# A two-layer graph kernel on one core: 32768 for the dynamic transfers' scratch, f32 one-hots, no room of its own for xin

## What is computed

```python
# layer 0: Z is x (12500, 256), U (4, 256, 16), Dmat (256, 256)
ZU = jnp.einsum('nd,kdr->knr', Z, U)
zs = ZU[:, src, :]
zd = ZU[:, dst, :]
logits = (zs * zd).sum(-1) / 4
seg_max = segment_max(logits, dst)              # per head
exp_l = jnp.exp(logits - seg_max[:, dst])
alpha = exp_l / (segment_sum(exp_l, dst)[:, dst] + 1e-16)
agg = segment_sum(alpha[..., None] * zs, dst)
w = jax.nn.softmax(head_w)
ssa = jnp.einsum('k,knr,kdr->nd', w, agg, U)
Z_half = 0.5 * Z + 0.5 * ssa
residual = Z_half - (Z_half @ Dmat.T) @ Dmat
x = layernorm(x + relu(Z_half + 0.5 * (residual @ Dmat) - 0.05))
# layer 1: xt = (x @ weight).reshape(-1, 4, 64); alpha from xt[row] and xt[col]
tmp = jnp.einsum('nh,nhd->nd', alpha[:n], xt[col[:n]])   # broadcast over the 4 heads
x = layernorm(x + broadcast(tmp))
```

## Time and profile before

| | |
|---|---|
| median of 3 runs | 3771.14 us (3765.44 to 3793.86) |
| the profiled execution | 3755.32 us, span 3753.5 us, mean granted clock 0.572 |
| PE busy | 1961.4 us (52%), 15249 products |
| PE's weight loads | 1492.6 us (40%) |
| DVE busy | 1919.1 us (51%) |
| ACT busy | 1169.7 us (31%) |
| POOL busy | 1721.7 us (46%) |
| prologue, edge loop | 0 to 178 us, 178 to 3301 us |
| dense stage, layer 1 | 3301 to 3412 us, 3412 to 3753 us |

### The profile page before, as it was taken

How to read it: one execution, slowest core, us unless ns; L and a number is a source line. 1 busy time by engine, 2 the same in 40 slices (tenths; PEclk the granted TensorE clock), 3 DMA queues, 4 the chain that set the end, 5 groups by cost and what they waited for, 6 DMA issues and landing times. The chain is left out here.

```text
span 3753.5 us, 61674 instructions
## 1 busy us (share of the span) xinstructions
PE 1961.4 (52%) x15249; PEld 1492.6 (40%) x15250; DVE 1919.1 (51%) x5861; ACT 1169.7 (31%) x3041; POOL 1721.7 (46%) x1833
## 2 busy tenths in 40 slices
PE   7344545454555445445445455354444554594776
PEld 7233434333343333333334334243333333453665
DVE  6344545445555445545455455455445544682566
ACT  2012222323323232323223232223232323353557
POOL 3544454444444444444444444544544444224662
PEclk8555555555555555555555555555555555597877
DMA  6211211121221212211112112121211121293343
GB/s 208 52 37 38 48 42 43 39 46 41 48 47 43 44 40 45 47 40 44 42 38 46 42 41 47 41 48 41 47 38 44 40 47 38 65 314 115 120 139 98
DMA packets 406592, 232.96 MB, mean 62 GB/s; under 512 B 284096, under 2 KB 371434, under 8 KB 406506
## 3 DMA queue, kind: packets, MB, share of 16 engines
q1 hardware_dynamic: 346666, 154.11, 15.0%
q0 software_dynamic: 59840, 77.87, 9.7%
HBM read 134.80 MB, written 42.55 MB: 47 GB/s over the span
## 5 line engine op out<-in xcount | busy, mean ns | idle before, releaser
L549 POOL DMA_INDIRECT arena<-z_table,sslot x1563 | 1487.8, 952 | 1702.9 <-SPq L400 1191.5
L1303 PE MATMUL bank<-arena 128*128 x4992 | 609.5, 228 | 564.2 <-issue 474.7
L1538 ACT ACTIVATE arena<-bank 128x272 f32<-128x272 f32 x416 | 268.4, 662 | 1614.6 <-remote 983.0
L1303 PEld LDWEIGHTS bank<-arena 128*128 128x128 bf16 x4992 | 469.3, 107 | 708.9 <-issue 616.4
L850 DVE TENSOR_TENSOR xin<-arena,bank 128x512 f32<-128x512 f32 x208 | 142.9, 687 | 1034.3 <-remote 697.3
L1515 ACT ACTIVATE acc<-xTb 128x68 f32 x1600 | 386.6, 312 | 350.1 <-issue 339.6
L1320 PE MATMUL bank<-xto,arena 128*128 128x68 bf16 x3328 | 330.7, 246 | 218.9 <-issue 218.8
L1320 PE MATMUL bank<-arena 128*128 128x68 bf16 x1664 | 300.3, 244 | 211.1 <-issue 135.0
L1320 PEld LDWEIGHTS bank<-xto,arena 128*128 128x128 bf16 x3328 | 284.7, 132 | 242.1 <-issue 241.7
L1291 PE MATMUL bank<-ident_b,arena 128*128 128x128 bf16 x1664 | 211.0, 306 | 317.9 <-remote 132.1
L841 DVE TENSOR_SCALAR arena<-iota_b,didx 128x128 bf16<-128x128 bf16 x1664 | 302.0, 264 | 40.8 <-issue 34.2
(11 more groups left out here) (250 smaller groups left out, 2493.2 us busy)
## 6 DMA issues: line engine op xcount, KB each, us to landing
arena<-arena SPq DMA_DIRECT2D x1660, 32.0 KB
arena<-z_table,sslot POOLq DMA_INDIRECT x1563
dspace<-in_xT SPq DMA_DIRECT2D x49, 256.0 KB
xmz_table<-agn SPq DMA_DIRECT2D x49, 256.0 KB
x_table<-arena SPq DMA_DIRECT2D x14, 896.0 KB, 4.9
arena<-in_x SPq DMA_DIRECT2D x13, 896.0 KB, 11.0
out<-arena SPq DMA_DIRECT2D x12, 896.0 KB
xin<-in_xT SPq DMA_DIRECT2D x8, 896.0 KB
```

The lines of the kernel that those rows point to most:

```text
L549: pool.indirect_dma_start(ring[:, e % RING, :], None, z_table, bass.IndirectOffsetOnAxis(ap=sslot[:, e:e + 1], axis=0)).then_inc(tiles_in[ ...
L1303: last = T.matmul(zd_ps[g % 2][:, u * KR:(u + 1) * KR], onehotT[:, g * G + u, :], z3[:, bass.ds(tiles[u], 1), s, :].rearrange("p a c -> p ...
L1538: A.activation(sums[:, :, 1 + q * Q:1 + (q + 1) * Q].rearrange("p c j -> p j c"), sum_ps[q % 2][:, 0:Q * AW].rearrange("p (j c) -> p j c", ...
```

## The change

- The program is built with 32768 for the scratch of dynamic transfers (SCRATCH) where it had its default of 16384.
- xin (2 x 7 x 256 f32 a partition) has no room of its own: its place is now in acc, `xq[0]` and `xq[1]` (xT tiles of the prologue) are in the ring and in the arena; prod, fwd, rev, xexp, eexp, fwd0, iota_i and attn move into other arrays. xmz_buf has four entries for six, and in the dense stage's loads `load_rows` comes in another order and behind sums_ps, `load_xmz` of groups 2 and 3 behind last_stored.
- One-hots and their transposes are f32. The transposes by PE read the upper bf16 halves of the f32 one-hots (`top(hot)`).
- Expansion and add-up are one f32 product a step where they were three in bf16. z is kept as f32 (zf, in the arena); z3, z_remainder, z_part, leave_rest and leave_low are gone. PE waits for zf_copied where it waited for z_rest, the add-up for weighted where it waited for parts_ready.

```diff
-ZP = 3
...
-XB = 6
+XB = 4
+SCRATCH = 32768
...
-    return ap.bitcast(BF16).rearrange("p j (c two) -> p j c two", two=2)[:, :, :, 1]
+    return ap.bitcast(BF16).rearrange("p (c two) -> p c two", two=2)[:, :, 1]
...
-        z3 = part((NT + 1) * ZP * KR // 2).bitcast(BF16).rearrange("p (t s c) -> p t s c", s=ZP, c=KR)
+        zf = part((NT + 1) * KR).rearrange("p (t c) -> p t c", c=KR)
+        onehot1g = part(G * P)
+        at[0] = NT * D + 4 - AW * (B + 1) - 2 * B * P
-        onehot = part(B * P).bitcast(BF16).rearrange("p (h j n) -> p h j n", h=2, j=B)
-        onehotT = part(B * P // 2).bitcast(BF16).rearrange("p (j e) -> p j e", j=B)
+        oflat_end = at[0] + 4 * S
+        onehot0 = part(B * P)
+        onehotT = part(B * P).rearrange("p (j e) -> p j e", j=B)
+        spare_at = at[0] - AW * (B + 1)
...
-        gT = acc[:, :, :].rearrange("p t c -> p (t c)")[:, 0:GB * 512].rearrange("p (r d) -> p r d", r=GB)
-        zf = acc[:, :, :].rearrange("p t c -> p (t c)")[:, 0:NT * KR].rearrange("p (t c) -> p t c", c=KR)
+        acc_flat = acc[:, :, :].rearrange("p t c -> p (t c)")
+        gT = acc_flat[:, 0:GB * 512].rearrange("p (r d) -> p r d", r=GB)
+        xin = acc_flat[:, GB * 512:GB * 512 + 2 * T7 * D].rearrange("p (h t d) -> p h t d", h=2, t=T7)
...
-        rest = xto_flat[:, 0:B * AW].rearrange("p (j c) -> p j c", c=AW)
-        low = xto_flat[:, B * AW:B * AW + B * AW // 2].bitcast(BF16).rearrange("p (j c) -> p j c", c=AW)
...
-        xin = sb("xin", [P, 2, T7, D])
-        xin_flat = xin[:, :, :, :].rearrange("p h t d -> p (h t d)")
-        xat = [AW * (B + 1)]
-        def xpart(width):
-            a = xin_flat[:, xat[0]:xat[0] + width]
-            xat[0] += width
-            assert xat[0] <= 2 * T7 * D
-            return a
-        prod = xpart(G * KR).rearrange("p (j c) -> p j c", j=G)
-        fwd0, fwd, rev0, rev, xexp, eexp = [xpart(P) for _ in range(6)]
+        onehot1 = (xto_flat[:, 0:(B - G) * P], onehot1g)
+        def hot(h, j):
+            if h == 0:
+                return onehot0[:, j * P:(j + 1) * P]
+            return onehot1[0][:, j * P:(j + 1) * P] if j < B - G else onehot1[1][:, (j - B + G) * P:(j - B + G + 1) * P]
+        prod = xto_flat[:, (B - G) * P:(B - G) * P + G * KR].rearrange("p (j c) -> p j c", j=G)
+        rev = sb("rev", [P, P])[:, :]
+        xexp = eexp = rev
-        state_a = arena[:, 4 * T7 * D:4 * T7 * D + AW * (B + 1)].rearrange("p (c j) -> p c j", c=AW)
+        state_a = arena[:, spare_at:spare_at + AW * (B + 1)].rearrange("p (c j) -> p c j", c=AW)
-        assert yat + S // 2 <= 2 * T7 * D
+        yat += S // 2
+        fwd = xTb_flat[:, yat:yat + P]
+        assert yat + P <= 2 * T7 * D
...
-        xq = [a.rearrange("p t d -> p (t d)").rearrange("p (c n) -> p c n", c=DC) for a in (xin[:, 0], xin[:, 1], xTb[:, 0], xTb[:, 1])]
+        fwd0 = rev0 = agn_flat[:, YT * D + 2 * P:YT * D + 3 * P]
+        xq = [a.rearrange("p (c n) -> p c n", c=DC) for a in (ring.rearrange("p r c -> p (r c)")[:, 0:T7 * D], arena[:, oflat_end:oflat_end + T7 * D])]
+        xq += [a.rearrange("p t d -> p (t d)").rearrange("p (c n) -> p c n", c=DC) for a in (xTb[:, 0], xTb[:, 1])]
...
-        xmz_buf = [xto[:, 0, :, 0:D], xto[:, 1, :, 0:D], xin[:, 0], xin[:, 1], xTb[:, 0], xTb[:, 1]]
+        xmz_buf = [xto[:, 0, :, 0:D], xto[:, 1, :, 0:D], xTb[:, 0], xTb[:, 1]]
...
-            for g in range(4):
+            sp.wait_ge(sums_ps, (B // Q) * (NB - 1))
+            for g in (0, 1, 2, 6, 9, 10):
...
-            for g in range(6, 8):
+            for g in (3, 4, 5, 7, 8):
-            for g in range(2, 4):
-                load_xmz(g)
-            for g in (4, 5, *range(8, NG7)):
+            for g in range(11, NG7):
-            for g in range(4, XB):
+            for g in range(2, XB):
...
-            def z_remainder(s, half):
-                dve.wait_ge(z_parts, 2 * half + s + 1)
-                if s == 0:
-                    dve.wait_ge(z_out[half], 16 * T7)
-                for t in range(half * NT // 2, (half + 1) * NT // 2, T7):
-                    part = slice(t, t + T7)
-                    to = zf[:, part, :] if s == 0 else z3[:, part, ZP - 1, :]
-                    last = V.tensor_tensor(to, zf[:, part, :], z3[:, part, s, :], ALU.subtract)
-                last.then_inc(z_rest, 1)
...
-                    last = V.tensor_scalar(onehot[:, h, j, :], iota_b[:, :], didx[:, h, j:j + 1], None, ALU.is_equal)
+                    last = V.tensor_scalar(hot(h, j), iota_b[:, :], didx[:, h, j:j + 1], None, ALU.is_equal)
...
-                def leave_rest(g):
-                    js = slice(g * G, (g + 1) * G)
-                    dve.wait_ge(weighted, NG * b + g + 1)
-                    V.tensor_tensor(rest[:, js, :], zs[:, h, js, :], top(zs[:, h, js, :]), ALU.subtract).then_inc(rest_ready, 1)
-                def leave_low(g):
-                    js = slice(g * G, (g + 1) * G)
-                    dve.wait_ge(rest_ready, NG * b + g + 1)
-                    V.tensor_tensor(low[:, js, :], rest[:, js, :], top(rest[:, js, :]), ALU.subtract).then_inc(parts_ready, 1)
-                weigh(0)
-                weigh(1)
-                if not first:
-                    dve.wait_ge(sums_ps, (B // Q) * b)
-                leave_rest(0)
-                weigh(2)
-                leave_rest(1)
-                leave_low(0)
-                weigh(3)
-                leave_rest(2)
-                leave_low(1)
-                leave_rest(3)
-                leave_low(2)
-                leave_low(3)
+                for g in range(NG):
+                    weigh(g)
...
-                    last = T.transpose(tr_ps[g % 2][:, u * P:(u + 1) * P], onehot[:, h, g * G + u, :], ident_b[:, :])
+                    last = T.transpose(tr_ps[g % 2][:, u * P:(u + 1) * P], top(hot(h, g * G + u)), ident_b[:, :])
...
-                    for s in range(ZP):
-                        last = T.matmul(zd_ps[g % 2][:, u * KR:(u + 1) * KR], onehotT[:, g * G + u, :],
-                                        z3[:, bass.ds(tiles[u], 1), s, :].rearrange("p a c -> p (a c)"), start=(s == 0), stop=(s == ZP - 1))
+                    last = T.matmul(zd_ps[g % 2][:, u * KR:(u + 1) * KR], onehotT[:, g * G + u, :],
+                                    zf[:, bass.ds(tiles[u], 1), :].rearrange("p a c -> p (a c)"), start=True, stop=True)
...
-                        pe.wait_ge(parts_ready, NG * b + q // 2 + 1)
-                    js = slice(q * Q, (q + 1) * Q)
-                    parts = (top(zs[:, h, js, :]), top(rest[:, js, :]), low[:, js, :])
+                        pe.wait_ge(weighted, NG * b + q // 2 + 1)
-                        for s in range(ZP):
-                            last = T.matmul(sum_ps[q % 2][:, (u % Q) * AW:(u % Q + 1) * AW], onehot[:, h, u, :], parts[s][:, u % Q, :],
-                                            start=(s == 0), stop=(s == ZP - 1))
+                        last = T.matmul(sum_ps[q % 2][:, (u % Q) * AW:(u % Q + 1) * AW], hot(h, u), zs[:, h, u, :], start=True, stop=True)
...
-            pe.wait_ge(z_rest, 4)
+            pe.wait_ge(zf_copied, NG7)
...
-            def z_part(s, half):
-                ts = slice(half * NT // 2, (half + 1) * NT // 2)
-                if s == 1:
-                    act.wait_ge(z_rest, 2 * half + 1)
-                else:
-                    act.wait_ge(zf_copied, (half + 1) * T7)
-                A.activation(z3[:, ts, s, :], zf[:, ts, :], ACT.Copy).then_inc(z_parts, 1)
-            for g in range(8):
+            for g in range(NG7):
-            z_part(0, 0)
-            for g in range(8, 11):
-                copy_z(g)
-            z_part(1, 0)
-            for g in range(11, NG7):
-                copy_z(g)
-            z_part(0, 1)
-            z_part(1, 1)
...
-    nc = bacc.Bacc("TRN2", target_bir_lowering=False, num_devices=1)
+    nc = bacc.Bacc("TRN2", target_bir_lowering=False, num_devices=1, dynamic_dma_scratch_size=SCRATCH)
```

More of the change, by code:

```diff
@@ L201, in program @@
         iota_row = sb("iota_row", [P, P])
-        iota_i = sb("iota_i", [P, P], I32)
+        iota_i = dst1
         stepno_i = sb("stepno_i", [P, SG], I32)
@@ L264, in program @@
         wx = sb("wx", [P, DC, WW])
-        attn = sb("attn", [1, 2 * HO])
+        attn = x1T_row
         hw = sb("hw", [1, 3, K])
@@ L304, in program @@
         x_in = [sem(f"x_in{i}") for i in range(len(xq))]
-        z_rest = sem("z_rest")
         weights_read = sem("weights_read")
@@ L328, in program @@
         x_ready, e_ready, ratio_ready, et_ready = sem("x_ready"), sem("e_ready"), sem("ratio_ready"), sem("et_ready")
-        z_parts, scale_ready = sem("z_parts"), sem("scale_ready")
-        weighted, rest_ready, parts_ready = sem("weighted"), sem("rest_ready"), sem("parts_ready")
+        scale_ready, weighted = sem("scale_ready"), sem("weighted")
         sums_ps, sums_copied, keep_ready, scan_done, state_stored = (
@@ L611, in _ @@
             V.memset(backx[0:1, P - K:P], NEG)
```

(6 more changed lines are left out.)

## The result

The changed kernel takes 3809.55 us (median of 20 runs, 3770 to 3853) where the kernel before takes 3769.61 (20 runs, 3751 to 3794); by the ratio it is 1.0066 of before, interval 1.004 to 1.0092, so about 25 us slower. The two medians lie further apart than that because the ratio leaves disturbed runs out. In a later comparison on a chip of the same kind the ratio was 1.0106 (1.007 to 1.0142). The forecast was 3697, 2% faster: the time is inside its range and on the wrong side.

A forecast was written before the change was run, and what follows sets the result against it. No engine fills the loop; gathers and slow stretches cost about 24 us a period. Terms of +0.5 - 1.1 - 1.0 + 0.3 = -1.3 us, times 50, and ends of -9 give -74: 3697 us, range 3480 to 3920.

The forecast's parts named there:

- the clock: PE in the loop's f32 streak: 1.2 GHz for 6.8 us, then 2.4 GHz, lower again after each slow stretch.
- the f32 work: Expansion and add-up around the long burst of gathers: 7.8 steps left after the slow stretch, L1340 1.0 us later, half counted, +0.5 us a period.
- the fewer records: Expansion before the shorter burst of gathers: 32 fewer PE instructions make the slow stretch begin later, -1.1 us a period.
- the split: DVE's subtractions L980 and L985 go, and with them PE's waits behind them: -1.0 us a period.
- (a): Rival, chance 0.27: PE stays at 1.2 GHz through the f32 streak and add-up; +2.8 us a period, 3902 us.
- the short burst: Expansion group just ahead of a slow stretch: 8 steps of 5 records for 9, -1.1 us a period.
- +0.3 between scan and x_ready (one-hots): DVE's f32 one-hots take about 0.02 us more each, 32 a period, half of it between scans of the chain.
- -5 for the prologue: Before the loop: z_remainder and z_part go, saving 5 us of ACT's 11.3, since gathers and tables are made beside them.
- -4 for the last period: Period without gathers: PE takes 18.4 us for 18.1 and loses waits of 4.6, so -4 us.
- four buffers are 32 us of cover: 0: Dense stage after the loop: four x-product buffers for six still cover the 11.0 us loads, no cost; without cover 11 us once.
- The onset in the long burst: Time from a 16-gather burst's first gather to the slow stretch: 4.9 us before, 6.4 expected after the change.
- the stock of 150 instructions: Some 150 issued instructions, which gathers keep from being refilled, last until the slow stretch; fewer PE records make it begin later.

The follow-up runs named there:

- the paced kernel: The changed kernel with POOL waiting, ahead of every fourth gather, until the gather before it has landed; 3097 us, 1.2209, on the chip without slow stretches.

## Why the prediction was wrong, step by step

**The step that failed is the clock, in the price of the f32 work.** The prediction took "6.8 us at the lower level, then the higher" from the prologue and counted 43.7 steps done before the slow stretch. The changed kernel runs f32 products for 15.4 us at 0.50 in that place, for 27.68 us in the last period, and only a quarter to a third of its f32 products in the loop are at the higher clock. Its first two terms, the f32 work and the fewer records, were +0.5 - 1.1 = -0.6 us a period. The runs have +1.7 to +2.0 for them: f32 for three bf16 products is +4.8 to +5.1 (1.0066 or 1.0106 less 0.9422, times 3755 us, over 50 periods), and the register instructions that go with it are -3.1 (155 us over 50). The miss of 2.3 to 2.6 a period is 115 to 130 us, and the split gave 20 of it back (-1.4 for -1.0); the sum was off by 99 to 114 (-74 against +25 and +40). That these 2.3 to 2.6 are the clock's doing is argued: no run had the same products at the higher clock.

**Why (a) came out too dear.** It is the rival with the lower clock throughout, and its first two terms are +2.9 + 0.6 = +3.5 for the +1.7 to +2.0 measured. A quarter to a third of the products had the higher clock after all, as the 32 in 3.88 us do in the short burst. The forecast and (a) did not leave the register instructions out: the 0.395 us of an expansion step before holds their pace. What neither had is their share on the path, 3.1 us a period, beside 5 for f32. The two large terms nearly cancel, and a sum of +0.5 and -1.1 did not show how much hung on each.

**Where the miss sits in the trace.** By place the forecast had +0.5 and -1.0 between the first copy and the next scan, and the two traces differ by -0.6 there: right. Its -1.1 between x_ready and the copies (the short burst) is -0.5; that term took the fewer records and gave the longer products nothing, though at the lower clock they are +1.7, as (a) had it. Its +0.3 between scan and x_ready (one-hots) is +1.5. With slow stretches this last segment is 17.6 to 18.7 us in the traces of the changed kernel and its variants, also with one bf16 product a step (18.7), and 15.6 to 16.9 in those of the kernel before and its variants: it goes with the other parts of the change and not with the f32 products. All 32 one-hots stand in it and not half of them, at 22 ns more each, 0.7 us; what the rest of the +1.5 is stays open. So the account by runs and the account by place do not name the same term, and which part of the miss the clock made is not settled.

**The ends were wrong too.** The forecast had -5 for the prologue, -4 for the last period and 0 for the dense stage, together -9. Between the two traces, the first product of the expansion comes 4.1 us earlier. The last period takes 7.7 us more from its first expansion product to the end of its add-up (47.4 and 55.1; in it are the 27.68 us at 0.50, where the forecast had the higher clock for the larger part). The dense stage takes 10.3 more. That is +14 for -9, so 23 of the 104 us between forecast and trace (+30 for -74) are not in the loop at all. The term "four buffers are 32 us of cover: 0" failed; its bound, "11 us once", is about what came.

**What held.** The split: -1.4 measured for -1.0. The duration of one-hots and their copies: 286 and 1009 ns. Register instructions of the f32 form: one a step. The prologue. The onset in the long burst: 7.5 us for 6.4 in the period shown, 8.2 in the median, 10.5 in (a). One reading was small by half a microsecond: the 43 products left before take 3.0 us, 1084.1 to L1340 at 1087.14, not 2.5. Another was too strong: bf16 work can go with the higher clock, since three bf16 products with one register instruction a step have 0.59 over the loop, more than the 0.54 of the f32 ones.

**What is not settled about the stock of 150 instructions.** Counted from a burst's first gather to the first 2 us with at most nine records, the kernel before has about 155 records (quartiles 150 and 157) in 4.7 us, so a fixed stock fits. The changed kernel has 118 in 8.2 us in the median, but with quartiles of 90 and 147 records and 6 and 10.4 us: a full stock would be its upper end, and nothing here says what fills it. The kernel with one product a step, some 70 records in 4 to 5 us, does not test it: in half of its bursts PE had issued nothing since the burst began. So a fixed number does not set the onset. What does is open, and so is why one kind of chip has these stretches; the paced kernel, which would have tested it, ran where there are none.

**Open**: what keeps PE at 1.2 GHz in a gap-free f32 streak. The operand's values are out where there are no slow stretches, and gathers are out by the last period; nothing else was tried.

## What to carry to other kernels

Before an f32 product replaces three bf16 ones, count what the sequencer issues for each and look at the spacing: here a register instruction per product cost 4% of the kernel where the slow stretches are, and leaving out a part of the numbers (two bf16 parts for three) gained 6% where f32 lost 1%. A clock that rose in one stage is no evidence for another; price f32 on PE at the lower clock and let the higher be the rival. Before buffers are taken from a later stage, measure that stage: here four for six cost 10 of the 30 us between the two traces. And measure on more than one chip: the change costs 0.7 to 1.1% on one kind and 4.2% on the other.

## What the runs showed of the hardware

Chips run the same program at 3754 and at 2537 us. On the first kind the sequencers of every engine but POOL's nearly stop for 18 us a period while gathers run; on the second they don't, with gathers of the same 944 ns. The granted clock stayed at 0.50 for 27.68 us in which PE was never idle and did f32 products alone. At that clock 24 bf16 products came in 3.03 us with a register instruction each, and in 1.28 with one for three.
